# Linear attention and mixture of experts: one of four key-value products moved from GpSimd to VectorE, the second norm's statistics from VectorE to ScalarE

## The chip, the cores and the metric

The kernel runs on one core of a Trainium2 chip. The metric is the time of one execution on the device in microseconds (us), the median of several runs. The engines are TensorE (PE), VectorE (DVE), ScalarE (ACT), GpSimd (POOL) and SyncE (SP), which issues DMAs.

## The reference

The input x is 16 sequences of 512 tokens of width 128, in float32. Layer 0 is a state-space recurrence and a top-1 mixture of experts; layer 1 is linear attention and a top-2 mixture of experts. Both edits lie in layer 1's attention and in the norm behind it:

```python
h = _layernorm(x) * (1 + ca) + sa
q = softplus(h @ Wq.T + bq); k = softplus(h @ Wk.T + bk); v = h @ Wv.T + bv   # 16 heads of 8
kv  = cumsum(k[:, :, :, None] * v[:, :, None, :], axis=1)
k1  = cumsum(k, axis=1)
out = einsum('zsD,zsDe->zse', q, kv) / sum(q * k1)
x = x + ga * (out @ Wo.T + bo)
h = _layernorm(x) * (1 + cb) + sb          # the second norm
x = x + gb * moe(h)                        # top 2 of 8 experts
```

## The kernel before

The program has five phases, one behind the other: set-up and the first layer's norm and gate; the recurrence; layer 1's attention (about 345 to 705 us of the profiled execution), into which the first layer's results come; the expert phase (to about 925 us); and a last join, parts of which are laid into the expert phase. Everything below is about the attention phase.

A sequence `w` is cut into C = 4 chunks of 128 tokens. The phase is a software pipeline over sequences: each engine has a written-out loop over `n`, and each piece of work in it is a function of a sequence, such as `weighted(n - 1, 0)`. An engine executes strictly in that order; `need(engine, name, count)` is a wait on a semaphore. For each sequence:

- ScalarE normalises x (`norm0`), TensorE turns it (`turned`) and makes queries, keys and values; ScalarE and VectorE together make softplus out of absolute value, exponential, logarithm and two additions. VectorE's `softplus` (line 2007) is the last of these and sets the semaphore `qk`.
- For each chunk `c`, the outer products of keys and values, a tensor `kv` of 128 tokens x (8 x 128), are made by GpSimd in `products(w, c)` (line 1641). A ring of KB = 3 buffers (`kvb`) holds them. TensorE forms their running sums over tokens in `sums(w, c)` (line 2450, a product with a triangular matrix of ones), and VectorE multiplies these with q in `weighted(w, c)` (line 1983); TensorE's `reduced(w, c)` adds over heads.
- `states` (TensorE, line 2567) and `prefixes` (VectorE, line 2027) make the sums carried from chunk to chunk; `denominators` (VectorE, line 1989) the reciprocals; `divided` (line 1974) the attention output `g_t`.
- `projected` and `back` return it to token order, VectorE's `residual` (line 2032) adds it to x and sets `x3`.
- The second norm: VectorE's `moments` (lines 2038 and 2044) takes mean and variance with the batch-norm instructions, ScalarE's `variance_log` and `variance_root` make the reciprocal root (in `rv`), VectorE's `shifted` the product of minus the mean and it, ScalarE's `normed` (line 1821) applies both, VectorE's `modulated` (lines 2057, 2059) the modulation; `gated` and `added` (line 2070) put the norm's result into x.
- ScalarE's `squares` (line 1803), `payload` (lines 1715, 1717) and `turned_pay` (line 1834, output `p_t`) prepare the rows for the experts. TensorE's `logits_back` (line 2616), VectorE's `logits`, `largest` and `chosen` (lines 2076 to 2111) pick the two experts, and GpSimd's `send` (line 1650) writes rows to the experts' lists by indirect DMAs, eight for each sequence, laid between the products.

In VectorE's loop `chosen(n - 5)` stands right ahead of `corrected(n)` and `softplus(n)`, for which TensorE's `states(n - 1)` waits. TensorE lays idle products (line 70) into waits when the pipeline fills and drains. When the last sequences have drained, `front_counts` and `front_rows` on VectorE plan the first expert tiles, SyncE loads these rows, and TensorE goes on with the expert phase.

Of the kernel before, what the change touches and what calls it, by code (L numbers as in the profile page):

```python
# [16 lines left out]
P = 128  # L17
D = 128
C = 4
# [18 lines left out]
def build(nc, a, out):  # L38
# [9 lines left out]
    with ctx:  # L48
# [1232 lines left out]
        with ExitStack() as sc:  # L1281
# [17 lines left out]
            st = sb("st", [P, C, 6], scope=sc)  # L1299
            mv = [sb(f"mv{j}", [P, C, 2], scope=sc) for j in range(2)]  # L1300
# [46 lines left out]
                     "exp", "u1", "cor", "sub", "ln", "qk", "kv", "tri", "qc", "red", "k1", "qd", "st_ps", "ds", "skv", "den", "rden", "den_out", "spread0", "spread1",  # L1347
                     "att", "fold_ps", "fold", "folded", "wo", "wo_t", "wo_ps", "x3", "st", "mv", "lv", "rs", "sh", "me", "rm", "normed", "cb", "h4", "sq",
# [134 lines left out]
            with nc.Block() as block:  # L1483
# [142 lines left out]
                def _(pool):  # L1626
# [27 lines left out]
                    for n in range(B + 6):  # L1654
                        send(n - 6, 6)
                        products(n, 0)
                        send(n - 6, 7)
                        send(n - 5, 0)
                        products(n, 1)
                        send(n - 5, 1)  # L1660
                        send(n - 5, 2)
                        products(n, 2)
                        send(n - 5, 3)
                        products(n, 3)
                        send(n - 5, 4)
                        send(n - 5, 5)
# [14 lines left out]
                def _(act):  # L1681
# [3 lines left out]

                    def variance_log(w):
                        if exists(w):
                            need(act, "init", 3)
                            need(act, "mv", w + 1)
# [55 lines left out]
                    def relu_keys(w):  # L1745
                        if exists(w):
                            need(act, "k_ps", w + 1)
                            need(act, "kv", C * (w - 1))
# [4 lines left out]
                    def values(w):  # L1753
                        if exists(w):
                            need(act, "v_ps", w + 1)
                            need(act, "kv", C * (w - 1))
# [81 lines left out]
                    for n in range(4, B + 8):  # L1838
# [15 lines left out]
                        payload(n - 7)  # L1854
                        turned_pay(n - 7)
# [57 lines left out]
                def _(dve):  # L1913
# [70 lines left out]

                    def denominators(w):
# [48 lines left out]
                    def moments(w):  # L2034
                        if exists(w):
                            need(dve, "x3", w + 1)
                            for c in range(C):
                                last = nc.vector.bn_stats(st[:, c, :], tile(w, c))
                            last.then_inc(s["st"], 1)
                            need(dve, "st", w + 1)  # L2040
                            need(dve, "lv", w - 1)
                            need(dve, "sh", w - 1)
                            for c in range(C):
                                last = nc.vector.bn_aggr(mv[w % 2][:, c, :], st[:, c, :])
                            last.then_inc(s["mv"], 1)

                    def shifted(w):
                        if exists(w):
                            need(dve, "rs", w + 1)
                            need(dve, "normed", w - 1)  # L2050
                            nc.vector.scalar_tensor_tensor(sh[w % 2][:, :], mv[w % 2][:, :, 0], -1.0, rv[w % 2][:, :], ALU.mult, ALU.mult).then_inc(s["sh"], 1)
# [137 lines left out]
                    for n in range(B + 5):  # L2189
                        weighted(n - 1, 0)  # L2190
                        denominators(n - 1)
                        correction(n)
# [14 lines left out]
                        moments(n - 2)  # L2207
# [191 lines left out]
                def _(pe):  # L2399
# [386 lines left out]
```

## Time and profile before

| | |
|---|---|
| time, median of 3 runs | 938.53 us (938.17 to 942.1) |
| the profiled execution | 945.22 us, span 943.4 us |
| PE busy | 858.5 us, 91% |
| VectorE busy | 774.1 us, 82% |
| ScalarE busy | 618.2 us, 66% |
| GpSimd busy | 566.4 us, 60% |
| GpSimd's products, line 1641 | 64 of them, 127.3 us, mean 1995 ns |

The profile is one execution. A row of the timeline gives start and duration in us; the shares of busy time are averages over all five phases, and PE is nearly full in most of them. A wait is printed in square brackets at the end of the row that ended it, with the engine and line that released it.

### The profile page before, as it was taken

To read this page: it belongs to the slowest core of one execution; us is meant where nothing else is said; L and a number is where in the kernel's file an instruction comes from. 1 tells how busy PE (TensorE), PEld (TensorE's weight loads), DVE (VectorE), ACT (ScalarE), POOL (GpSimd) and SP (SyncE) were. 2 spreads that over 40 slices of the span, in tenths; PEclk is the share of its full clock that TensorE was granted. 3 is DMA by queue.
4 is the path that set the end of the run, shared out by engine and by line. 5 is a ranking of instruction groups with operands and counts; after the bars stand their busy time and mean duration, and the time that the engine had idled before them with its cause. 6 is when DMAs were issued, how large, how long until landed. Compare 5 with 4: busy or idle time off the path is not lost.

```text
span 943.4 us, 24125 instructions
## 1 busy us (share of the span) xinstructions
PE 858.5 (91%) x7676; PEld 674.7 (72%) x7692; DVE 774.1 (82%) x2369; ACT 618.2 (66%) x1603; POOL 566.4 (60%) x547
## 2 busy tenths in 40 slices
PE   6979898998999989999999999999879999999990
PEld 5945576645445458888778877787668888888890
DVE  3988787999999736988999999999886866666996
ACT  3557123487888446467677777666557888888880
POOL 1211004277776414443888888888777777777773
PEclk9989999899999999999999999999998999999996
DMA  5330262233223203001111112111227766756987
GB/s 155 95 95 1 67 204 59 104 110 141 102 101 130 99 3 96 15 17 35 43 52 49 49 54 64 53 50 49 66 68 219 219 183 183 228 181 196 338 263 248
DMA packets 93962, 105.82 MB, mean 112 GB/s; under 512 B 16095, under 2 KB 75802, under 8 KB 91661
## 3 DMA queue, kind: packets, MB, share of 16 engines
q1 hardware_dynamic: 81884, 84.59, 29.3%
q0 software_dynamic: 8640, 17.97, 5.3%
q10 hardware_dynamic: 3312, 1.70, 0.6%
q8 instruction: 64, 1.05, 0.5%
q14 instruction: 62, 0.50, 0.2%
HBM read 79.91 MB, written 24.32 MB: 110 GB/s over the span
## 4 chain that ended last, share of the span: by engine, by line
PE 48%; DVE 8%; issue 2%; ACT 2%; DMA 2%; POOL 1%; SPq 0%; ACTq 0%; DVEq 0%; POOLq 0%
PE ps L2694 12%; PE ps L2450 10%; PE ps L2717 6%; PE ps L2466 2%; PE ps L2513 2%; PE ps L2441 2%; PE ps L2416 2%; PE ps L2677 2%; PE ps L2567 2%; PE ps L2551 2%; PE ps L2429 1%; DVE qk L2001 1%; DVE qk L2007 1%; PE ps L2461 1%; DMA parts<-gx,dest 1%
## 5 line engine op out<-in xcount | busy, mean ns | idle before, releaser
L1641 POOL TENSOR_TENSOR kvb<-qk,v 128x1024 f32<-128x1024 f32 x64 | 127.3, 1995 | 68.8 <-DVE qk L2007 48.9
L1650 POOL DMA_INDIRECT rows_of<-payb,posu x128 | 144.3, 1128 | 40.1 <-issue 27.5
L2450 PE MATMUL ps<-con,kvb 128*128 128x128 f32 x1024 | 126.0, 276 | 0.0
L1161 PE MATMUL ps<-masked,ew 128*128 128x512 f32 x256 | 123.3, 610 | 1.9 <-DVE masked L1091 1.8
L2450 PEld LDWEIGHTS ps<-con,kvb 128*128 128x128 f32 x1024 | 119.4, 192 | 1.0 <-issue 1.0
L2378 DVE TENSOR_SCALAR qk<-ps,b 128x256 f32<-128x256 f32 x142 | 62.1, 478 | 49.7 <-PE ps L2694 44.6
L1674 POOL DMA_INDIRECT parts<-h,dest x72 | 80.6, 1119 | 23.3 <-issue 20.1
L1674 POOL DMA_INDIRECT parts<-gx,dest x70 | 78.7, 1125 | 21.3 <-issue 19.2
L1091 DVE TENSOR_TENSOR masked<-f_t,wide 128x512 f32<-128x512 f32 x128 | 85.9, 715 | 4.9 <-PE ps L1161 4.7
L1983 DVE TENSOR_TENSOR qc<-ps,qk 128x1024 f32<-128x1024 f32 x64 | 78.0, 1218 | 9.3 <-PE ps L2450 8.2
L1161 PEld LDWEIGHTS ps<-masked,ew 128*128 128x128 f32 x256 | 44.8, 192 | 44.9 <-issue 30.0
L2717 PE MATMUL ps<-w,f_t 128*128 x568 | 75.1, 275 | 0.0
L2717 PEld LDWEIGHTS ps<-w,f_t 128*128 128x128 f32 x568 | 69.0, 192 | 8.2
L1888 ACT ACTIVATE qk<-ps,b 128x256 f32<-128x256 f32 x142 | 59.6, 470 | 18.3 <-PE ps L2694 17.9
L2694 PE MATMUL ps<-qd,ex 128*128 128x256 f32 x288 | 69.8, 386 | 0.0
L2694 PE MATMUL ps<-qd,lg 128*128 128x256 f32 x280 | 66.2, 379 | 0.0
L70 PE MATMUL ps<-con 128*128 128x128 f32 x398 | 56.3, 293 | 5.5 <-PEq L75 3.9
L70 PEld LDWEIGHTS ps<-con 128*128 128x128 f32 x398 | 51.4, 204 | 9.6 <-issue 6.8
L2694 PEld LDWEIGHTS ps<-qd,ex 128*128 128x128 f32 x288 | 53.0, 194 | 6.0
L1893 ACT ACTIVATE nrm<-qk,limit 128x512 f32<-128x512 f32 x71 | 51.3, 722 | 6.8
L2267 DVE SCALAR_TENSOR_TENSOR f_t<-qk,nrm 128x512 f32<-128x512 f32 x71 | 49.2, 693 | 6.8 <-DVE qk L2378 0.5
L2694 PEld LDWEIGHTS ps<-qd,lg 128*128 128x128 f32 x280 | 50.5, 190 | 5.4
(370 smaller groups left out, 2107.0 us busy)
## 6 DMA issues: line engine op xcount, KB each, us to landing
wide<-hot_dram SPq DMA_DIRECT2D x16, 1024.0 KB, 4.6
kvb<-rows_of SPq DMA_DIRECT2D x71, 132.0 KB, 2.5
ex<-in_w_dram SPq DMA_DIRECT2D x36, 256.0 KB
lg<-in_w_dram SPq DMA_DIRECT2D x35, 256.0 KB
toep<-taps_dram SPq DMA_DIRECT2D x16, 512.0 KB, 4.5
xg<-parts SPq DMA_DIRECT2D x16, 512.0 KB, 5.2
x_tok<-in_x_dram SPq DMA_DIRECT2D x16, 256.0 KB, 2.9
rb<-den_dram SPq DMA_DIRECT2D x64, 64.0 KB
```

The costliest lines, as they stand in the source:

```text
L70: nc.tensor.matmul(ps[:, bank, 0:P], k("ident"), k("ident"), start=True, stop=True)
L1091: nc.vector.tensor_tensor(masked[e % 4][:, :], f_t[w % W][:, :], wide[w % W][:, e, :], ALU.mult).then_inc(s["masked"], 1)
L1161: nc.tensor.matmul(ps[:, w % 2, :], ew0[:, e, :], masked[e % 4][:, :], start=False, stop=(e == E - 1)).then_inc(s["product"], 1)
L1641: nc.gpsimd.tensor_tensor(kv[g % KB][:, :, :].rearrange("p e (h d) -> p e h d", h=H), k_in, v_in, ALU.mult).then_inc(s["kv"], 1)
L1650: nc.gpsimd.indirect_dma_start(rows_of, bass.IndirectOffsetOnAxis(ap=posu[w % PR][:, slot, t:t + 1], axis=0), pay[w % PB][:, t, :], None). ...
L1674: nc.gpsimd.indirect_dma_start(parts, bass.IndirectOffsetOnAxis(ap=dest[:, at, c:c + 1], axis=0), yw[u][:, c, :], None).then_inc(s_out[u], 16)
L1888: last = nc.scalar.activation(glu[v % 2][:, f, :], ps[:, bank, f * SP:(f + 1) * SP], ACT.Relu, bias=b1[:, bass.ds(e * NF + f, 1)], scale=-1.0)
L1983: nc.vector.tensor_tensor(qc[g % 2][:, :, :], cum(g), q_in, ALU.mult).then_inc(s["qc"], 1)
L2378: last = nc.vector.tensor_scalar(lin[v % 2][:, f, :], ps[:, bank + 1, f * SP:(f + 1) * SP], b1[:, bass.ds(e * NF + 2 + f, 1)], 8.0, ALU.ad ...
L2450: last = nc.tensor.matmul(cum(g)[:, e, :], kv[g % KB][:, e, :], k("upto"), start=True, stop=True)
L2694: last = nc.tensor.matmul(ps[:, bank + f // 2, (f % 2) * SP:(f % 2 + 1) * SP], w1c[v % WC][:, f * P:(f + 1) * P], x_t[v % 2][:, :], start= ...
L2717: last = nc.tensor.matmul(to, act_t[v % 2][:, j, c * P:(c + 1) * P], w2[:, bass.ds(e * (2 * D) + j * D, D)], start=False, stop=(c == S - 1 ...
```

## The change

GpSimd no longer makes the product of a sequence's fourth chunk. VectorE makes it in a new function `last_product(w)`, with a semaphore `kv_last` of its own, one round later in the loops' count, between `denominators` and `correction`. VectorE's `moments` is removed. In its place ScalarE gets three functions behind `payload` and ahead of `turned_pay`: `row_sums` (four copies that also give their sum), `negative_means` (one small scaling) and `centred_squares` (four squares of x minus mean that also give their sum, the bias being an operand by partition). `variance_log` and `shifted` read these results.

```diff
@@ GpSimd's loop
                         products(n, 2)
                         send(n - 5, 3)
-                        products(n, 3)
                         send(n - 5, 4)
...
@@ ScalarE
+                    def row_sums(w):
+                        if exists(w):
+                            need(act, "x3", w + 1)
+                            need(act, "nm", w)
+                            need(act, "vs", w)
+                            for c in range(C):
+                                last = nc.scalar.activation(unread[:, c, :], tile(w, c), ACT.Copy, accum_out=sx[:, c:c + 1])
+                            last.then_inc(s["sx"], 1)
+
+                    def negative_means(w):
+                        if exists(w):
+                            need(act, "sx", w + 1)
...
+                            nc.scalar.activation(nm[w % 2][:, :], sx[:, :], ACT.Copy, scale=-1.0 / D).then_inc(s["nm"], 1)
+
+                    def centred_squares(w):
+                        if exists(w):
+                            need(act, "nm", w + 1)
+                            need(act, "lv", w - 1)
+                            for c in range(C):
+                                last = nc.scalar.activation(unread[:, c, :], tile(w, c), ACT.Square, bias=nm[w % 2][:, c:c + 1], accum_out=vs[w % 2][:, c:c + 1])
+                            last.then_inc(s["vs"], 1)
...
-                            nc.scalar.activation(rv[w % 2][:, :], mv[w % 2][:, :, 1], ACT.Ln, bias=eps[:, :]).then_inc(s["lv"], 1)
+                            nc.scalar.activation(rv[w % 2][:, :], vs[w % 2][:, :], ACT.Ln, bias=eps[:, :], scale=1.0 / D).then_inc(s["lv"], 1)
...
                         payload(n - 7)
+                        row_sums(n - 5)
+                        negative_means(n - 5)
+                        centred_squares(n - 5)
                         turned_pay(n - 7)
                         norm0(n)
@@ VectorE
+                    def last_product(w):
+                        if exists(w):
+                            c = C - 1
+                            g = w * C + c
+                            need(dve, "qk", w + 1)
+                            need(dve, "v", w + 1)
+                            need(dve, "tri", g - KB + 1)
...
+                            nc.vector.tensor_tensor(kv[g % KB][:, :, :].rearrange("p e (h d) -> p e h d", h=H), k_in, v_in, ALU.mult).then_inc(s["kv_last"], 1)
...
                         weighted(n - 1, 0)
                         denominators(n - 1)
+                        last_product(n - 1)
                         correction(n)
                         weighted(n - 1, 1)
...
                         weighted(n - 1, 3)
-                        moments(n - 2)
                         first_cum(n)
@@ TensorE, in sums(w, c)
-                            need(pe, "kv", g + 1)
+                            if c == C - 1:
+                                need(pe, "kv_last", w + 1)
+                            else:
+                                need(pe, "kv", (C - 1) * w + c + 1)
```

The order of instructions on VectorE in one steady round, before, from the fourth product with q (`weighted(n - 1, 3)`) to the logits (`qd` is `first_cum`, `h` is `modulated`, `g_t` is `divided`, `rden` is `denominators`, `ex` is `correction`):

```order
L1983 TENSOR_TENSOR qc<-ps,qk 128x1024
L2038 BN_STATS st<-x_tok 128x6 x4
L2044 BN_AGGR mv<-st 128x2 x4
L2013 TENSOR_TENSOR qd<-ps,qk 128x512
L2070 TENSOR_TENSOR x_tok<-x_tok,gx 128x512
L2027 TENSOR_TENSOR skv<-skv 128x144 x2
L2057 TENSOR_TENSOR h<-h,rows 128x512
...
L1983 TENSOR_TENSOR qc<-ps,qk 128x1024
L1989 RECIPROCAL rden<-ps 96x128
L1994 SCALAR_TENSOR_TENSOR ex<-lg,ex 128x1024
L1983 TENSOR_TENSOR qc<-ps,qk 128x1024
```

And the same piece with the change, where line 2024 is the new product and the lines of the others have moved:

```order
L2013 TENSOR_TENSOR qc<-ps,qk 128x1024
L2054 TENSOR_TENSOR qd<-ps,qk 128x512
L2098 TENSOR_TENSOR x_tok<-x_tok,gx 128x512
L2068 TENSOR_TENSOR skv<-skv 128x144 x2
L2085 TENSOR_TENSOR h<-h,rows 128x512
...
L2013 TENSOR_TENSOR qc<-ps,qk 128x1024
L2030 RECIPROCAL rden<-ps 96x128
L2024 TENSOR_TENSOR kvb<-qk,v 128x1024
L2035 SCALAR_TENSOR_TENSOR ex<-lg,ex 128x1024
L2013 TENSOR_TENSOR qc<-ps,qk 128x1024
```

The eight small instructions of the moments are gone, and one large product stands between the reciprocal and the softplus correction. On ScalarE, the piece from the payload to `normed` (`h`), with the change:

```order
L1740 ACTIVATE payb<-h,rm 128x128 x4
L1742 ACTIVATE payb<-place 128x4
L1693 ACTIVATE unread,sx<-x_tok 128x128 x4
L1701 ACTIVATE nm<-sx 128x4
L1708 ACTIVATE unread,vs<-x_tok,nm 128x128 x4
L1861 ACTIVATE p_t<-ps 128x512
L1748 ACTIVATE nrm<-x_tok,shift,rs 128x128 x4
L1755 ACTIVATE ex<-ps,bq 128x512
L1848 ACTIVATE h<-x_tok,sh,rv 128x128 x4
```

Before, `p_t` followed directly on `payb<-place`; nine activations now stand between the two.

## Rows read from the trace of the kernel before

**Rows 1.** Chain of waits, 546 to 570 us: start, duration, what

```profile
550.55 0.97 PE ps L2567 x6
...
558.63 1.79 PE ps L2450 x16
...
565.49 0.12 PE ps L2616
...
569.51 1.24 DVE qk L2007
```

**Rows 2.** Timeline of VectorE, 546 to 570 us: start, duration, instruction

```profile
549.18 1.22 DVE L2007 TENSOR_TENSOR qk<-qk,lg 128x1024 f32<-128x1024 f32 x1
550.32 0.68 DVE L2032 TENSOR_TENSOR x_tok<-x_tok,ps 128x512 f32<-128x512 f32 x1
...
555.18 0.86 DVE L2038 BATCH_NORM_STATS2 st<-x_tok 128x6 f32<-128x128 f32 x4
...
556.37 0.66 DVE L2013 TENSOR_TENSOR qd<-ps,qk 128x512 f32<-128x512 f32 x1
556.95 0.93 DVE L2070 TENSOR_TENSOR x_tok<-x_tok,gx 128x512 f32<-128x512 f32 x1
...
558.36 0.68 DVE L2057 TENSOR_TENSOR h<-h,rows 128x512 f32<-128x512 f32 x1
...
560.46 1.23 DVE L1983 TENSOR_TENSOR qc<-ps,qk 128x1024 f32<-128x1024 f32 x1
...
562.46 1.16 DVE L1994 SCALAR_TENSOR_TENSOR ex<-lg,ex 128x1024 f32<-128x1024 f32 x1
564.12 1.22 DVE L1983 TENSOR_TENSOR qc<-ps,qk 128x1024 f32<-128x1024 f32 x1 [0.50 <-PE ps L2450]
565.64 0.19 DVE L2076 TENSOR_TENSOR logit<-ps,gb 128x32 f32<-128x32 f32 x1 [0.30 <-PE ps L2616]
...
566.27 0.25 DVE L2090 TENSOR_TENSOR wts<-top 128x4 f32<-128x4 f32 x1
```

**Rows 3.** Timeline of ScalarE, 546 to 570 us

```profile
549.74 0.19 ACT L1717 ACTIVATE payb<-place 128x4 f32<-128x4 f32 x1
553.91 0.60 ACT L1834 ACTIVATE p_t<-ps 128x512 f32<-128x512 f32 x1 [3.99 <-PE ps L2538]
...
556.52 1.64 ACT L1821 ACTIVATE h<-x_tok,sh,rv 128x128 f32<-128x128 f32 x4
...
564.68 0.30 ACT L1803 ACTIVATE junk<-h 128x128 f32<-128x128 f32 x1
...
564.97 0.30 ACT L1803 ACTIVATE junk<-h 128x128 f32<-128x128 f32 x1
```

**Rows 4.** Timeline of GpSimd, 546 to 570 us

```profile
555.33 1.99 POOL L1641 TENSOR_TENSOR kvb<-qk,v 128x1024 f32<-128x1024 f32 x1
...
560.05 1.98 POOL L1641 TENSOR_TENSOR kvb<-qk,v 128x1024 f32<-128x1024 f32 x1
562.20 2.28 POOL L1650 DMA_INDIRECT rows_of<-payb,posu  x1 [0.17 <-issue]
564.50 1.99 POOL L1641 TENSOR_TENSOR kvb<-qk,v 128x1024 f32<-128x1024 f32 x1
```

**Rows 5.** Timeline of VectorE and of TensorE, first sequence

```profile
373.37 1.23 DVE L2007 TENSOR_TENSOR qk<-qk,lg 128x1024 f32<-128x1024 f32 x1
...
374.74 0.97 PE L2567 MATMUL ps<-v,qk 128*128 128x144 f32 x6
```

**Rows 6.** Timeline of VectorE and ScalarE in the drain

```profile
681.27 0.68 DVE L2032 TENSOR_TENSOR x_tok<-x_tok,ps 128x512 f32<-128x512 f32 x1
...
683.29 1.64 ACT L1821 ACTIVATE h<-x_tok,sh,rv 128x128 f32<-128x128 f32 x4
...
685.12 0.68 DVE L2057 TENSOR_TENSOR h<-h,rows 128x512 f32<-128x512 f32 x1
```

**Rows 7.** Windows: busy us of PE, PEld, DVE, ACT, POOL; clock, DMA share, GB/s

```profile
705.00:710.00 5.00, 3.97 (x22) 3.34 (x21) 1.79 (x10) 0.99 (x2) 3.78 (x5) 0.68 0.79 227
```

More of the change, by code:

```diff
@@ L1298, in build @@
             rows = [sb(f"rows{u}", [P, 3, D], scope=sc) for u in range(W)]
-            st = sb("st", [P, C, 6], scope=sc)
-            mv = [sb(f"mv{j}", [P, C, 2], scope=sc) for j in range(2)]
+            sx = sb("sx", [P, C], scope=sc)
+            nm = [sb(f"nm{j}", [P, C], scope=sc) for j in range(2)]
+            vs = [sb(f"vs{j}", [P, C], scope=sc) for j in range(2)]
+            unread = sb("unread", [P, C, D], scope=sc)
             ms = [sb(f"ms{j}", [P, C], scope=sc) for j in range(2)]
@@ L1346, in build @@
             names = ("weights", "slots", "heads", "split", "init", "nrm0", "turned", "feat", "k_ps", "q_ps", "v_ps", "v", "abs_k", "abs_q", "relu_k", "relu_q",
-                     "exp", "u1", "cor", "sub", "ln", "qk", "kv", "tri", "qc", "red", "k1", "qd", "st_ps", "ds", "skv", "den", "rden", "den_out", "spread0", "spread1",
-                     "att", "fold_ps", "fold", "folded", "wo", "wo_t", "wo_ps", "x3", "st", "mv", "lv", "rs", "sh", "me", "rm", "normed", "cb", "h4", "sq",
+                     "exp", "u1", "cor", "sub", "ln", "qk", "kv", "kv_last", "tri", "qc", "red", "k1", "qd", "st_ps", "ds", "skv", "den", "rden", "den_out", "spread0", "spread1",
+                     "att", "fold_ps", "fold", "folded", "wo", "wo_t", "wo_ps", "x3", "sx", "nm", "vs", "lv", "rs", "sh", "me", "rm", "normed", "cb", "h4", "sq",
                      "pay", "pay_ps", "pay_t", "gx", "x4", "lg_ps", "lg_t", "lg_back", "lg", "max", "idx", "idf", "hot", "ed", "ee", "e1", "p1", "taken", "counted", "carried",
@@ L1747, in relu_keys @@
                             need(act, "k_ps", w + 1)
-                            need(act, "kv", C * (w - 1))
+                            need(act, "kv", (C - 1) * (w - 1))
+                            need(act, "kv_last", w - 1)
                             need(act, "st_ps", w - 1)
@@ L1755, in values @@
                             need(act, "v_ps", w + 1)
-                            need(act, "kv", C * (w - 1))
+                            need(act, "kv", (C - 1) * (w - 1))
+                            need(act, "kv_last", w - 1)
                             need(act, "st_ps", w - 1)
@@ L2032, in residual @@
                             nc.vector.tensor_tensor(seq(w), seq(w), ps[:, BACK, :].rearrange("p (c d) -> p c d", c=C), ALU.add).then_inc(s["x3"], 1)
[L2034 to L2045, printed above, removed]
                     def shifted(w):
@@ L2050, in shifted @@
                             need(dve, "normed", w - 1)
-                            nc.vector.scalar_tensor_tensor(sh[w % 2][:, :], mv[w % 2][:, :, 0], -1.0, rv[w % 2][:, :], ALU.mult, ALU.mult).then_inc(s["sh"], 1)
+                            nc.vector.tensor_tensor(sh[w % 2][:, :], nm[w % 2][:, :], rv[w % 2][:, :], ALU.mult).then_inc(s["sh"], 1)
                     def modulated(w):
```

6 lines of the change are left out of this document (5 added, 1 removed).

## The prediction

> **What bounds the kernel now.** The change touches only the attention phase, so I read the chain of waits there first, over one steady sequence [rows 1, 2]. It runs in a ring of two engines. VectorE finishes the softplus of a sequence (line 2007, at 549.18 and again at 569.51: a period of 20.33 us); TensorE, which has waited for it, starts at 550.55 and runs without a stop to its product of line 2616, which ends at 565.61 (15.06 us); VectorE takes the logits at 565.64 and needs 5.27 us until TensorE can start again. The sum is the period. TensorE and VectorE are thus both nearly full and neither is the bound alone: what counts is whether VectorE stands ready at 565.64.
>
> VectorE's own rows of that period [rows 2] show what room it has there. It takes the first product with q (line 1983) at 560.46, just behind the prefix sums that TensorE ended at 558.63 + 1.79 = 560.42, so that start is set by TensorE. It takes `ex` (line 1994) at 562.46 until 563.62, waits 0.50 us, takes the next line 1983 from 564.12 to 565.34, and waits 0.30 us for line 2616. Instructions that wait for nothing start 0.08 us before the end of the one before (line 2007 takes 1.22, and line 2032 starts 1.14 behind it), so each wait hides 0.08 more. The room is 0.50 + 0.30 + 2 x 0.08 = 0.96 us.
>
> **VectorE: the product it takes over.** `last_product` stands between the reciprocal and `ex`, inside that room. The trace has no such product on VectorE; the nearest row is line 2007, as many elements (128x1024 float32) with both inputs in SBUF: 1.22 us, 1.14 from start to start. Bounds: 1.07 (1.14 less the 0.07 by which such rows differ) and, if the inner broadcast cost as much as GpSimd's same product [rows 4], 1.98. I take 1.14, since line 1983 also reads a broadcast input at 1.23. The excess over the room is 1.14 - 0.96 = 0.18 us.
>
> **GpSimd: the product it loses.** It stood at 564.50 to 566.49 [rows 4]. VectorE's small subtraction of line 2090, two SBUF inputs, began at 566.27, took 0.25 and ended at 566.52, just behind it; where nothing of GpSimd's runs the same line takes 0.17. So the chain gets 0.08 us back. Nothing else waited for GpSimd there: TensorE uses this fourth product only in its next round. Steady cost: 0.18 - 0.08 = 0.10 us a period, over ten such periods 1.0 us. Bounds: with a product of 1.07 the cost is 0.03 us a period, 0.3 in all; with no cost at all the 0.08 would be a gain of 0.8; with 1.98 it is 1.98 - 0.96 - 0.08 = 0.94 a period, 9.4 us, which I leave out of the range, since line 1983's broadcast costs nothing to see.
>
> **VectorE: the moments it loses.** Start of line 2038 to start of line 2013 is 556.37 - 555.18 = 1.19 us [rows 2]. They would be a gain if VectorE set its own pace there, but behind them stands line 2070, two SBUF inputs. It already took 0.93 where a like op takes 0.68, ending at 557.88, 0.56 behind the end of GpSimd's second product at 555.33 + 1.99 = 557.32 [rows 4]. Without the moments it would stand ready at 555.76, wait for that same end and finish at the same 557.9. Line 2057 then starts at 558.36 as before, and the line 1983 at 560.46 waits for TensorE in any case. Worth: 0. I weighed a page here. The Trainium skill, page "SBUF — State Buffer", section "Who interferes with whom", says that a VectorE instruction with two SBUF inputs and a GpSimd instruction that reads SBUF hold one port in turn, one fully blocking the other. By it VectorE gains nothing from the moments' going; without it the 1.19 us would still be stopped by TensorE at 560.42. This trace agrees, in the 0.93 and the 0.25.
>
> **ScalarE: the statistics it takes over.** Its place is behind the payload copies, where it idles 3.99 us until 553.91 [rows 3]. The residual that it now needs ends at 550.32 + 0.68 = 551.00 [rows 2]. Four accumulating copies at the pace of line 1803 (564.68 to 564.97, 0.29 each) plus the last accumulator read: 1.26 us. One small scaling, as line 1717: 0.19, with 0.03 us of signal on either side. Four centred squares with a bias by partition: line 1821 has bias and scale by partition and goes at (1.64 - 0.10) / 4 = 0.385 each without an accumulator, line 1803 has neither and goes at 0.29 with one, of which the read is 0.09; half of 0.385 - 0.20 for the one operand gives 0.29 + 0.09 = 0.38 each, 1.52. Bounds for the four: 1.17 and 1.9. All together 3.04 us: 551.04 + 3.04 = 554.08, 0.17 behind the old 553.91. Line 1821 then ends at 558.16 + 0.17 = 558.33, and VectorE's line 2057 started at 558.36. Cost 0, cover 0.03 there and 0.10 more before 560.46; with 1.9 instead of 1.52 it would be about 0.25 us a period, 2.5 us. (The Trainium skill, page "ScalarE: Activation LUTs", section "What ACT_TABLE_LOAD costs", gives 93 ns for each operand by partition; by that the squares are 0.38 too.)
>
> **The first sequences** run at 18 us, TensorE being full. Only the first is tight: softplus ends at 374.60 and TensorE starts its next piece at 374.74 [rows 5]. VectorE waits 0.50 (+0.08) there, so 1.14 - 0.58 = 0.56 us is lost. In sequences two to five VectorE ends about 1 us early, but ScalarE's 3.04 us then stand in front of `norm0` and `normed`. I take 0.85 us for them together, by carrying 0.56 on; bounds 0 and 4 x 0.56. Sum 1.4 us.
>
> **The drain.** Behind the last sequence the pipeline empties in one chain, and ScalarE is on it. The last residual runs from 681.27 to 681.95; ScalarE's line 1821 for the sequence before starts at 683.29, and VectorE's line 2057, which waits for it, at 685.12 [rows 6]. Now the 3.04 us stand in between: 681.98 + 3.04 = 685.02, then p_t (0.5), line 1821 from 685.5 to 687.15, line 2057 at 687.2. That is 2.0 us later, and everything to the start of the expert phase hangs on it. The moments, 1.2 us of VectorE just ahead of 684.5, go, but ScalarE is the later of the two. One sequence earlier ScalarE idled and nothing is lost.
>
> **Sum.** 1.4 + 1.0 + 2.0 = 4.4 us. The profiled execution took 945.22 us with a span of 943.4; it becomes 949.6. It lies 6.7 us over the median of the three runs, 938.53; the shift goes over unchanged: **942.9 us**. A difference below 0.5% (4.7 us) can hardly be told from none, and this sum lies right under it.
>
> **Rivals.**
> 1. The clock falls in the drain. TensorE's granted clock was 0.68 in 705 to 710 [rows 7], shortly behind a wait of over 2 us. In the drain there is now a wait of 2.5 us, from about 683.2 to 685.7, where there was 0.33. If the clock goes to 1.2 GHz there, the 18 filler products (2.17 us, 0.97 us of idle behind them) take twice as long and push the chain by 1.2 us; a shifted fall at the start of the expert phase adds or takes up to 1.7. Against it: the clock was full all through 660 to 705 with gaps of 1 us. Time 944 to 946. Chance 0.17.
> 2. The steady period loses more than 0.1. Either the product on VectorE meets GpSimd's third product, which ends at 560.05 + 1.98 = 562.03, only 0.43 us ahead of its place at 562.46; or ScalarE is late by more than 0.30. Speaking for it: GpSimd's send at 562.20 took 2.28 us beside `ex`, against about 1 us, so such meetings occur. Each 0.3 us a period is 3 us: 946 to 950. Chance 0.16.
> 3. Other side: all is hidden. If VectorE's product costs 1.07 and TensorE's waits in the first sequences absorb the shift, only the drain is left, and there the moments' 1.2 us are partly gained: 938.5 to 940.5. Chance 0.15.
> 4. Faster: GpSimd sends without a pause behind 667. If its queue, 2 us shorter by a product, let the expert phase start its row writes earlier and these bounded the end, 936.5. Against it, TensorE runs that whole phase without a wait. Chance 0.04. That the change would leave the instructions as they were is excluded by their order.
>
> The sum's own case has 0.48, and 941.3 to 944.3 around it; about 0.17 of these 0.48 lies over 943.2 (938.5 + 4.7). So slower 0.17 + 0.16 + 0.17 = 0.50, faster 0.04 and within 0.46. The range takes the sum's case, the clock and half of rivals 2 and 3: 939.8 to 947.5.
>
> **What would show it.** The new trace should have VectorE's product at about 1.23 us; no wait ahead of the two q products behind it; steady softplus starts 20.43 us apart; `moments` gone and line 2070's successor waiting for GpSimd, some 1.5 us long; ScalarE's idle of 3.99 down to about 1.1 (up to the residual) and none at p_t; in the drain p_t near 2.2 us later against the residual than before. The prediction is wrong if the period falls below 20.3 or exceeds 20.7, or if the drain from the last softplus to the expert phase grows by less than 1 us or more than 4.

## The result, and the profile after

The changed kernel took 947.58 us, the median of 20 runs (941.21 to 955.18); the kernel before, run beside it, 941.31 us, also of 20 (938.17 to 949.8). The ratio is 1.0056 with a 95% interval of 1.0034 to 1.0077: 5.3 us slower, between 3.2 and 7.2. The two medians lie 6.3 us apart; all differences below are by the ratio, to which the interval belongs. The changed kernel's profiled execution took 943.13 us with a span of 941.3, less than the profiled one before. That is no gain of the change: attention began at 339.05 us in it against 345.05 before, so the phases ahead, which are the same code, ran 6.0 us shorter in that one execution. From there to the end it took 3.9 us longer. The kernel before was 938.53 us over the three runs that the prediction had, and 941.31 over twenty, so the forecast has to be read as a difference: 4.4 us over 938.53. The ratio on that base gives 943.8.

The shares of the page after (engine, busy us, instructions):

```profile
PE 853.6 (91%) x7676; PEld 672.9 (71%) x7692; DVE 787.3 (84%) x2257; ACT 665.6 (71%) x1875; POOL 556.0 (59%) x531
```

VectorE is 13 us busier although it lost the moments, ScalarE 47, and GpSimd only 10 less busy although 16 products of 2 us are gone. Windows tell more than the whole span. 460 to 560 us, kernel before, then after (busy us of PE, PEld, DVE, ACT, POOL; clock, DMA share, GB/s):

```profile
460.00:560.00 100.00, 94.55 (x1022) 79.71 (x1026) 93.81 (x260) 73.18 (x199) 85.51 (x60) 1.00 0.18 54
```

```profile
460.00:560.00 100.00, 93.92 (x1030) 79.48 (x1037) 98.03 (x220) 87.81 (x276) 85.27 (x55) 1.00 0.18 53
```

VectorE went from 93.8% to 98.0%. Its timeline of one period after, to be read against [rows 2] (start, duration, instruction):

```profile
551.70 2.10 DVE L2098 TENSOR_TENSOR x_tok<-x_tok,gx 128x512 f32<-128x512 f32 x1
...
554.38 0.69 DVE L2085 TENSOR_TENSOR h<-h,rows 128x512 f32<-128x512 f32 x1
...
556.38 1.23 DVE L2013 TENSOR_TENSOR qc<-ps,qk 128x1024 f32<-128x1024 f32 x1
557.52 0.94 DVE L2030 RECIPROCAL rden<-ps 96x128 f32<-96x128 f32 x1
558.38 1.16 DVE L2024 TENSOR_TENSOR kvb<-qk,v 128x1024 f32<-128x1024 f32 x1
559.46 1.21 DVE L2035 SCALAR_TENSOR_TENSOR ex<-lg,ex 128x1024 f32<-128x1024 f32 x1
560.59 1.21 DVE L2013 TENSOR_TENSOR qc<-ps,qk 128x1024 f32<-128x1024 f32 x1
561.73 0.18 DVE L2104 TENSOR_TENSOR logit<-ps,gb 128x32 f32<-128x32 f32 x1
...
562.35 0.17 DVE L2118 TENSOR_TENSOR wts<-top 128x4 f32<-128x4 f32 x1
```

No row has a bracket: the waits of 0.50 and 0.30 us are gone. The new product starts 1.08 us ahead of `ex`, and `ex`, which used to be followed by a wait, now takes 1.13 from start to start. The chain of waits says the same in its own way. Before it went to and fro between TensorE and VectorE [rows 1]; after, over the same stretch, it never leaves VectorE (start, length, what):

```profile
554.38 0.70 DVE h L2085
...
557.52 0.94 DVE rden L2030
558.46 1.08 DVE kvb L2024
559.54 1.13 DVE ex L2035
560.67 1.14 DVE qc L2013
...
565.55 0.42 DVE qk L2048
```

ScalarE's and TensorE's timelines after, against [rows 3] and the TensorE start in [rows 1]:

```profile
545.52 0.20 ACT L1742 ACTIVATE payb<-place 128x4 f32<-128x4 f32 x1
546.95 0.31 ACT L1693 ACTIVATE unread<-x_tok 128x128 f32<-128x128 f32 x1 [1.23 <-DVE x_tok L2073]
...
548.26 0.20 ACT L1701 ACTIVATE nm<-sx 128x4 f32<-128x4 f32 x1
548.50 0.40 ACT L1708 ACTIVATE unread<-x_tok,nm 128x128 f32<-128x128 f32 x1
...
550.05 0.58 ACT L1861 ACTIVATE p_t<-ps 128x512 f32<-128x512 f32 x1
```

```profile
546.47 0.97 PE L2598 MATMUL ps<-v,qk 128*128 128x144 f32 x6 [1.02 <-DVE qk L2048]
```

The statistics take 546.95 to 550.05, 3.10 us. Counted from TensorE's start, `p_t` came at 553.91 - 550.55 = 3.36 before and comes at 550.05 - 546.47 = 3.58 now: 0.22 late, and without a wait.

GpSimd after, against [rows 4]:

```profile
551.26 1.98 POOL L1643 TENSOR_TENSOR kvb<-qk,v 128x1024 f32<-128x1024 f32 x1
...
558.12 3.41 POOL L1652 DMA_INDIRECT rows_of<-payb,posu  x1 [0.17 <-issue]
...
564.39 1.95 POOL L1652 DMA_INDIRECT rows_of<-payb,posu  x1 [0.30 <-issue]
```

The drain after, against [rows 6], ScalarE, VectorE and TensorE; then the windows' row of 683 to 686:

```profile
682.34 0.57 ACT L1861 ACTIVATE p_t<-ps 128x512 f32<-128x512 f32 x1
682.82 1.63 ACT L1848 ACTIVATE h<-x_tok,sh,rv 128x128 f32<-128x128 f32 x4
684.55 0.69 DVE L2085 TENSOR_TENSOR h<-h,rows 128x512 f32<-128x512 f32 x1 [3.26 <-ACT h L1848]
683.06 0.66 PE L2635 MATMUL ps<-p_t,gw 128*32 128x128 f32 x8 [2.59 <-ACT p_t L1861]
```

```profile
683.00:686.00 3.00, 2.94 (x19) 2.59 (x20) 1.41 (x3) 2.01 (x7) 2.39 (x3) 0.50 0.17 51
```

The last residual starts at 678.53, so line 2085 follows it by 6.02 us, against 685.12 - 681.27 = 3.85 before.

### The profile page after: what moved, and what is told of

It is laid out like the page before. It is cut to its first block, busy times and chain, and to the rows that moved or that the text cites. A ratio compares the mean times of both kernels' runs of the same rounds, so it can differ in the third digit from the quotient of the medians.

```text
span 941.3 us, 24269 instructions
## 1 busy us (share of the span) xinstructions
PE 853.6 (91%) x7676; PEld 672.9 (71%) x7692; DVE 787.3 (84%) x2257; ACT 665.6 (71%) x1875; POOL 556.0 (59%) x531
## 4 chain that ended last, share of the span: by engine, by line
PE 31%; DVE 22%; issue 4%; ACT 3%; DMA 2%; SPq 0%; POOL 0%; DVEq 0%; ACTq 0%; POOLq 0%
PE ps L2725 13%; PE ps L2748 6%; DVE qc L2013 4%; PE ps L2481 3%; DVE x_tok L2098 2%; DVE qk L2042 2%; PE ps L2708 2%; DVE ex L2035 2%; DVE kvb L2024 1%; DVE rden L2030 1%; DVE qk L2048 1%; PE ps L2497 1%; DVE h L2085 1%; DVE idx L2120 1%; DMA parts<-gx,dest 1%
## 5 line engine op out<-in xcount | busy, mean ns | idle before, releaser
L1652 POOL DMA_INDIRECT rows_of<-payb,posu x128 | 165.9, 1296 | 42.6 <-issue 29.6
L1643 POOL TENSOR_TENSOR kvb<-qk,v 128x1024 f32<-128x1024 f32 x48 | 95.0, 1988 | 80.4 <-DVE qk L2048 79.8
L1918 ACT ACTIVATE qk<-ps,b 128x256 f32<-128x256 f32 x142 | 59.7, 471 | 16.5 <-PE ps L2725 15.9
```

The lines of the kernel that those rows point to most:

```text
L1643: nc.gpsimd.tensor_tensor(kv[g % KB][:, :, :].rearrange("p e (h d) -> p e h d", h=H), k_in, v_in, ALU.mult).then_inc(s["kv"], 1)
L1652: nc.gpsimd.indirect_dma_start(rows_of, bass.IndirectOffsetOnAxis(ap=posu[w % PR][:, slot, t:t + 1], axis=0), pay[w % PB][:, t, :], None). ...
L1918: last = nc.scalar.activation(glu[v % 2][:, f, :], ps[:, bank, f * SP:(f + 1) * SP], ACT.Relu, bias=b1[:, bass.ds(e * NF + f, 1)], scale=-1.0)
```

## The experiments

To compare executions whose clock fell at different moments I cut each trace at the same instructions of the attention phase. The table is worked out from the timelines; each kernel has 4 to 12 runs behind its ratio (the changed one 20), beside 11 to 28 of the kernel before. **Five** is from the first softplus to the sixth. **Period** is a tenth of the time from the sixth to the sixteenth. **Drain** is from the last residual's start to the start of the `modulated` line behind it. For the whole periods between 450 and 680 us, per period: **waits** of VectorE and of TensorE on another engine, and **held**, which adds up, over VectorE's instructions, what each took beyond the shortest duration that the same one has in any of these traces, where that is over 0.1 us.

| kernel | five | period | drain | V waits | V held | T waits | median us | ratio (95%) |
|---|---|---|---|---|---|---|---|---|
| before | 88.45 | 20.35 | 3.85 | 0.80 | 0.39 | 0.92 | | |
| after | 89.74 | 20.47 | 6.02 | 0.00 | 1.56 | 1.04 | 947.58 | 1.0056 (1.0034 to 1.0077) |
| e1 | 90.04 | 20.47 | 6.03 | 0.00 | 1.56 | 1.04 | 945.05 | 1.0043 (1.0019 to 1.0068) |
| e2 | 89.78 | 20.47 | 3.86 | 0.00 | 0.42 | 1.06 | 943.81 | 1.0022 (0.9990 to 1.0054) |
| e3 | 89.13 | 20.35 | 6.03 | 0.80 | 1.56 | 0.92 | 944.82 | 1.0056 (1.0026 to 1.0087) |
| e4 | 90.07 | 20.47 | 3.83 | 0.00 | 1.56 | 1.04 | 947.85 | 1.0082 (1.0053 to 1.0112) |
| e5 | 88.46 | 20.25 | 6.03 | 0.80 | 1.57 | 0.82 | 942.14 | 1.0003 (0.9972 to 1.0034) |
| e6 | 96.54 | 24.63 | 6.03 | 2.24 | 2.11 | 3.32 | 993.47 | 1.0517 (1.0457 to 1.0577) |
| e7 | 86.04 | 29.97 | 5.32 | 6.73 | 4.38 | 8.44 | 1047.35 | 1.1145 (1.1096 to 1.1193) |
| e8 | 87.93 | 28.56 | 6.04 | 5.46 | 4.52 | 7.45 | 1029.61 | 1.0945 (1.0901 to 1.0988) |
| e9 | 85.98 | 22.59 | 3.86 | 0.42 | 3.34 | 2.18 | 967.21 | 1.0271 (1.0228 to 1.0313) |
| e10 | 88.74 | 22.93 | 6.03 | 0.21 | 3.84 | 2.27 | 971.63 | 1.0310 (1.0269 to 1.0351) |
| e11 | 86.72 | 22.47 | 6.04 | 0.65 | 3.84 | 2.04 | 965.32 | 1.0247 (1.0208 to 1.0286) |
| e12 | 90.06 | 23.08 | 6.03 | 0.45 | 4.13 | 2.65 | 972.59 | 1.0316 (1.0272 to 1.0360) |

For the kernels in the old order a second table cuts the same traces at two more places. **Last** is from the sixteenth softplus to the last residual, **packed** from that `modulated` line to the packed places (`packs`, VectorE's last step in planning the first expert tiles), **all** from the first softplus to the packed places.

| kernel | last | packed | all | against before |
|---|---|---|---|---|
| before | 30.41 | 16.95 | 343.16 | |
| after | 31.15 | 16.88 | 348.52 | +5.36 |
| e1 | 29.72 | 17.10 | 347.59 | +4.43 |
| e2 | 29.99 | 16.87 | 345.18 | +2.02 |
| e3 | 30.34 | 16.85 | 345.80 | +2.64 |
| e4 | 29.67 | 20.00 | 348.25 | +5.09 |
| e5 | 29.58 | 16.88 | 343.44 | +0.28 |

### e1_both, e2_product_only, e3_stats_only: the two parts apart

e1 is the changed kernel again. e2 keeps VectorE's product and gives VectorE its moments back; e3 keeps ScalarE's statistics and gives GpSimd its fourth product back.

```diff
  e2, ScalarE and VectorE          e3, GpSimd and VectorE
-     row_sums(n - 5)            +     products(n, 3)
-     negative_means(n - 5)      -     last_product(n - 1)
-     centred_squares(n - 5)
+     moments(n - 2)
```

> The changed kernel once more, beside the runs below. Theory: the attention phase alone grows, by parts that are the same in every execution: first sequences +0.5 to 1, ten steady periods of 20.45 us against 20.33 (+1.2), the drain +2.1; what lies over that is the granted clock, which falls at other places in each execution. So the softplus starts stand 20.45 apart again, and the time from the last residual to VectorE's modulation in the drain is 6.0 us against 3.85. Rival: the 6.0 us of the last drain were the fall of the clock seen there, and come out near 4 where the clock stays full.

> Only the product moves from GpSimd to VectorE; the moments stay on VectorE. Theory (a port wait takes the place of the moments, and TensorE sets the start of the first product with q anyway): the same period of 20.45, the first sequence +0.55, the drain as before (3.85 us from the last residual to the modulation); in all +1.5 to 2.5 us. Rival (the moments' 1.19 us are a real gain on VectorE that pays for the product): a period near 21.4 and over +10 us.

> Only the statistics move from VectorE to ScalarE; the product stays on GpSimd. Theory: period 20.33 unchanged although VectorE has 1.2 us less to do, first sequences +0.3 to 0.8 by norm0 and normed behind the statistics, drain +2.1; in all +2.5 to 3. Rival (VectorE's load sets the period): below 20.0 us a period, over 3 us faster in all.

The traces separate the parts more sharply than the times do. The product alone makes the whole 0.12 us of the period and 1.3 us of the first five sequences, and leaves the drain as it was. The statistics alone leave the period exactly as it was, cost 0.7 us in the first five and 2.2 us in the drain. Together the three stretches come to 1.3 to 1.6, 1.2 and 2.2, about 4.8 us. The last sequences give some back: "last" is 0.7 us shorter than before in e1. It is shorter wherever GpSimd makes no fourth product and the clock stays full (29.58 to 29.99 in e1, e2, e4 and e5, but 30.34 in e3). In all e1's trace is 4.43 us longer, and the parts alone 2.02 + 2.64 = 4.66. Beside them stand the measured 5.3 (3.2 to 7.2) and, for e1, 4.0 (1.8 to 6.4). The parts don't add up stretch by stretch: in the first five sequences e2 loses 1.33 us and e3 0.68, and both together 1.29 and 1.59. So e1 lost more there than the 0.5 to 1 that I expected, and e2 more than 0.55.

The trace after shows a price that e1's does not. TensorE waits 1.45 us for the last softplus in it and 1.46 in e1. Windows' rows just behind that wait, after and then e1:

```profile
649.00:651.00 2.00, 2.00 (x11) 1.91 (x11) 1.87 (x4) 1.70 (x10) 1.84 (x2) 0.50 0.00 0
```

```profile
651.00:653.00 2.00, 2.00 (x21) 2.00 (x20) 1.97 (x10) 1.94 (x12) 1.84 (x2) 1.00 0.00 0
```

The granted clock fell to 0.50 in one and stayed full in the other, with the same kernel, and "last" is 31.15 us against 29.72. So 1.4 of the 5.36 us of the trace after go with a fall of the clock that came in one execution and not in the other.

The statistics also settle what became of the moments. VectorE's second norm sum, in the groups by line of 460 to 620 us, e2 (moments there) and e3 (moments gone), each: count | busy, mean ns of one | idle before:

```profile
L2082 DVE TENSOR_TENSOR x_tok<-x_tok,gx 128x512 f32<-128x512 f32 x7 | 6.5, 935 | 0.0
```

```profile
L2097 DVE TENSOR_TENSOR x_tok<-x_tok,gx 128x512 f32<-128x512 f32 x8 | 16.8, 2104 | 0.0
```

It grew by 1.17 us when 1.19 us ahead of it went. In the trace after it stands over GpSimd's product of 551.26 to 553.24 and ends at 553.80, 0.56 us behind that product's end, as before. This is the rule that the prediction weighed (the Trainium skill, "SBUF — State Buffer", section "Who interferes with whom"), and e3 bears out the hold. Whether TensorE's prefix sums would have stopped the gain without it, as the prediction also says, no run separates.

### e4_drain_fixed: the statistics elsewhere in the drain

```diff
-                        row_sums(n - 5)
-                        negative_means(n - 5)
-                        centred_squares(n - 5)
+                        if n < B + 3:
+                            statistics(n - 5)
                         turned_pay(n - 7)
...
                         normed(n - 6)
+                        if n >= B + 3:
+                            statistics(n - 5)
```

> The changed kernel, but for the last two sequences ScalarE makes the statistics behind normed instead of ahead of p_t. Theory: the drain goes back to 3.9 to 4.2 us from the last residual to the modulation, everything behind it about 2 us earlier; the steady period stays 20.45; in all +2 to 3.5 us against before. Rival (the drain's length is the clock's or TensorE's): no change against the changed kernel.

`modulated` came back to 3.83 us behind the residual, but the stretch from there to the packed places was 20.00 us against 16.88 after: the same 3 us of ScalarE now stand ahead of its logit transpose. Nothing was won: the whole is +5.09 us against e1's +4.43, not 2 us less as expected, and the measured 7.7 us (5.0 to 10.5) says no better. In both places that I tried in the drain, ScalarE's queue is the path.

### e5_no_fourth, e6_two_products: no product, and two

```diff
  e5                                    e6, in last_product
-     last_product(n - 1)             +     nc.vector.tensor_tensor(again[w % 2] ..., k_in, v_in, ALU.mult)
                                            nc.vector.tensor_tensor(kv[g % KB] ..., k_in, v_in, ALU.mult)
```

> This kernel is the changed one with the fourth product made by no engine. TensorE's cumulative sums of every sequence's last chunk read what the buffer held before, so the output leaves out that chunk's own key-value products; every other instruction stands. Theory (the product on VectorE costs its own 1.08 us at a point of the ring, where all but some 0.96 us of it is hidden): softplus starts come 20.25 to 20.35 us apart (changed kernel 20.47, kernel before 20.35), so 0.12 to 0.22 less per period, and the first sequences win back the 0.5 to 1.3 us that the product alone took. In all 2 to 4 us less than the changed kernel, about 941 to 943 us. Rival (what costs is not the product but GpSimd's changed order of sends and products, or ScalarE's statistics): the periods stay 20.45 to 20.5.

> The changed kernel with VectorE's product made twice, the second time into a buffer that nothing reads. Theory (the room behind the product is used up by the first one, so that VectorE's further work lengthens the ring one for one): the period grows by the product's own 1.08 to 1.13 us, to 21.55 to 21.6 from 20.47, and the kernel is 16 to 19 us slower than the changed one, about 962 us. Rival (room left, the 0.12 us of the changed kernel come from meetings with GpSimd's work): the period grows by 0.1 to 0.5 us only, 2 to 8 us in all.

e5 came out as expected: 20.25. Without any fourth product VectorE's waits are back (0.80 a period), and the period is 0.10 below that of the kernel before, which is the small subtraction that GpSimd's fourth product used to hold up. So the two steady terms stand apart: e3 to e5 is GpSimd's product going, -0.10; e5 to e1 is VectorE's product coming, +0.22. In its first five sequences e5, with the statistics, loses nothing (88.46); the 0.68 us of e3 come only with GpSimd's fourth product beside them.

e6 missed by far. I expected 1.1 us a period and got 4.16. The second product took its 1.1, and everything behind it moved against GpSimd and ScalarE. Timeline of VectorE, then of TensorE, in e6, and its windows' row of 463 to 682:

```profile
587.10 2.95 DVE L2087 TENSOR_TENSOR h<-h,rows 128x512 f32<-128x512 f32 x1 [1.19 <-ACT h L1849]
```

```profile
577.81 1.78 PE L2600 MATMUL ps<-v,qk 128*128 128x144 f32 x6 [3.24 <-DVE qk L2050]
```

```profile
463.00:682.00 219.00, 187.94 (x1841) 159.21 (x1838) 194.04 (x413) 159.51 (x502) 162.48 (x99) 0.91 0.15 44
```

The sum of `modulated` now waits for ScalarE and is then held for 2.3 us by GpSimd's product; held time grew by 0.55 us a period against the changed kernel. TensorE waited 3.24 us in one piece, and the mean clock was 0.91 where it was 1.00 before. The line behind that wait took 1.78 us instead of 0.97. Of the 4.16 us, 1.1 are the product, 0.55 is held time, and the other 2.5 go with new waits and the lower clock, which I did not take apart. VectorE, "full" at 98%, did not simply get longer by what was added.

### e7_ring_before, e8_ring_after: a new order

```diff
@@ VectorE, from the logits on
+ corrected(n)  softplus(n)  residual(n - 2)  weighted(n - 1, 2)  states(n)  shifted(n - 3)  weighted(n - 1, 3)
  largest(n - 5)  chosen(n - 5)  gated(n - 4)  ...  modulated(n - 3)
+ ranked(n - 5)  placed(n - 5)
@@ TensorE
- states(n - 1)  ranks(n - 6)  sums(n - 2, 3)
+ states(n - 1)  sums(n - 2, 3)  ...  reduced(n - 2, 3)  ranks(n - 6)  keys(n)
```

> The kernel before with its loop's steps in another order: VectorE does the corrections, softplus, residual, weighting and shifts ahead of the choice of experts, ScalarE's weighing stands behind the queries' relu, TensorE's rank product behind the third reduction, GpSimd's sends one place later. What is computed is the same. Theory (the period is a ring of 15.06 us of TensorE and 5.27 us of VectorE, and part of VectorE's share is work that nobody in the ring waits for): the period falls to what TensorE's own work makes it, 19.3 to 19.8 us, and the kernel is 7 to 16 us faster, 925 to 934 us. Rival (VectorE's and GpSimd's load, or the sends' new places, hold the period): it stays 20.2 to 20.5 and the time within 3 us of the kernel before, or grows, if a new wait ends up in the ring.

> The same new order with both parts of the change in it. Theory (the change costs because its product lies in the ring): with the ring shorter than VectorE's and TensorE's own work, the product costs nothing or gains a little, 0 to 0.1 us a period against the same order without the change, and what is left is ScalarE's statistics in the drain, about 2 us: 0 to 3 us slower than that kernel. Rival (VectorE is the next to set the period, busy near 17 us of 20): the change costs 0.5 us or more per period there too, 5 us or more in all beside the drain's 2 us.

Neither theory: 30 us a period. In e7's trace TensorE waits twice:

```profile
569.54 0.18 PE L2586 MATMUL ps<-taken,earlier 128*128 128x32 bf16 x1 [3.58 <-DVE upto_now L2107]
574.61 0.61 PE L2414 MATMUL ps<-bk,one 128*128 128x512 bf16 x1 [4.87 <-DVE rank L2120]
```

I had moved the choice of experts behind work that nobody waited for, but TensorE's rank product stood ahead of its keys, and the keys need the bank that VectorE's `rank` empties. The ring became nearly all of both engines in turn. e8 is still of use: in that order the change gains 1.4 us a period (29.97 to 28.56), because VectorE's moments stood in the ring there and the product in VectorE's waiting time. That account is read from the order and the waits (VectorE's went from 6.73 to 5.46 us a period); no run took the two parts of the change apart in this order.

### e9_swap_before, e10_swap_after, e11_swap_stats: a smaller exchange

```diff
@@ VectorE                         @@ TensorE               @@ GpSimd: sends one product later
- largest(n - 5)  chosen(n - 5)    - ranks(n - 6)           - send(n - 6, 6) ahead of products(n, 0)
  corrected(n)  softplus(n)          sums(n - 2, 3)         + send(n - 6, 6), send(n - 6, 7) behind it
+ largest(n - 5)  chosen(n - 5)    + ranks(n - 6)           + send(n - 5, 0) behind products(n, 1) ...
```

> The kernel before with three places exchanged, the computation the same: VectorE makes the corrections and softplus ahead of the largest logits and the choice of experts, TensorE's rank product stands behind the fourth cumulative sums instead of ahead of them, and GpSimd's sends stand one product later. Unlike the first new order, the choice stays ahead of everything that TensorE waits for next. Theory (a ring of 15.06 us of TensorE and 5.27 us of VectorE, of which about 2.4 us are the choice, which the ring needs not): TensorE's 0.9 us wait ahead of the states goes, and the period falls from 20.35 to what either engine has of its own work, 20.33 - 0.89 = 19.4 of TensorE and 20.33 - 0.80 = 19.5 of VectorE: 19.5 to 19.8 us, the kernel 8 to 14 us faster than the one before. Rival (the exchange puts a wait in another place, as the first new order did): 20.3 us or more, no faster.

> The changed kernel with the same three places exchanged. Theory one (the product costs by its place in the ring): once the ring is loosened, it costs next to nothing, the period is 19.5 to 19.9 and the kernel 8 to 14 us faster than the changed one. Theory two (VectorE is full: in the changed kernel it is 98% busy from 460 to 560 us and waits for nobody, so that its own 20.4 us set the period, not the ring): the exchange takes nothing off, the period stays 20.2 to 20.5, and the kernel is 10 us or more slower than the one before with the exchange.

> The kernel before with the statistics by ScalarE alone, the fourth product on GpSimd, and the same three places exchanged. Theory (VectorE's floor is 19.5 us less the 1.24 us of the moments, so TensorE's 19.4 us are next): a period of 19.4 to 19.6, up to 0.2 us below that of the kernel before with the exchange, 0 to 3 us less in all, of which the 2.2 us that the statistics cost in the last sequences go off again. Rival (what the moments leave on VectorE is lost to the lock with GpSimd's product, as at the second norm's sum in the kernel before's order): the same period as the kernel before with the exchange, and 2 us slower in all.

TensorE's wait for softplus did go, and the first five sequences became 2.5 us shorter (88.45 to 85.98). But the period rose to 22.6. Groups by line in e9, 460 to 620 us, VectorE and TensorE:

```profile
L2070 DVE TENSOR_TENSOR x_tok<-x_tok,gx 128x512 f32<-128x512 f32 x7 | 15.2, 2178 | 0.0
L2090 DVE TENSOR_TENSOR wts<-top 128x4 f32<-128x4 f32 x7 | 12.3, 1755 | 0.2
```

```profile
L2538 PE MATMUL ps<-con,payb 128*128 128x128 f32 x32 | 5.6, 301 | 17.0 <-DVE rank L2120 17.0
```

The subtraction of line 2090, four elements a partition, now meets GpSimd's first product and takes 1.76 us instead of 0.17; the norm's sum 2.18. VectorE is held 3.3 us a period, its `rank` comes late, and TensorE waits for it 17.0 us in eight periods. With the change, or its statistics alone, in that order (e10, e11) the periods are 22.93 and 22.47, outside every range that I had given, and the times within 5 us of e9's. The hold only moved: in e11 the norm's sum takes 0.68 us, and the prefix additions behind it, which also read SBUF twice, are held instead:

```profile
L2067 DVE TENSOR_TENSOR skv<-skv 128x144 f32<-128x144 f32 x14 | 18.3, 1304 | 0.2
```

A pair of them takes 2.64 us where it is 0.64 elsewhere. Taking the moments away gained 0.12 us a period (22.59 to 22.47), and VectorE is held 3.84 us in e10 and e11 against 3.34 in e9.

### e12_second_early: GpSimd's second product one send earlier

```diff
                         send(n - 6, 7)
-                        send(n - 5, 0)
                         products(n, 1)
+                        send(n - 5, 0)
```

> The changed kernel with GpSimd's second product one send earlier, ahead of the send that waits for the places; nothing else is touched. In the changed kernel this product lies over VectorE's sum behind the second norm (x_tok with gx, both in SBUF), which takes 2.10 us there instead of about 0.68. Theory (VectorE is full and its own work, this hold of 1.4 us in it, sets the period of 20.47): the product ends before the sum starts, the sum takes 0.7 to 1.0 us, VectorE's waits come back (0.5 to 1.4 us a period), and the period is the ring's again, 20.25 to 20.35: 1.2 to 2.2 us less in ten periods and 2 to 4 us less in all. Rival (the product on VectorE adds to the ring by its place, whatever else VectorE does): the sum shortens but the period stays at 20.45 to 20.5.

The sum behind the second norm fell to what was expected, and the period rose all the same. VectorE in e12, 460 to 620 us:

```profile
L2098 DVE TENSOR_TENSOR x_tok<-x_tok,gx 128x512 f32<-128x512 f32 x7 | 4.7, 675 | 0.0
...
L2163 DVE SCALAR_TENSOR_TENSOR payb<-wts,payb 128x4 f32<-128x4 f32 x7 | 17.3, 2475 | 0.0
...
L2085 DVE TENSOR_TENSOR h<-h,rows 128x512 f32<-128x512 f32 x7 | 13.3, 1901 | 2.3 <-ACT h L1848 2.3
```

The product no longer holds the sum (0.68 us); in its new place it holds a four-element instruction that writes the payload (2.48 us), and `modulated` (1.90). 4.13 us a period are held where it was 1.56, and TensorE's waits rose from 1.04 to 2.65. Neither the expected 20.25 to 20.35 nor the rival's 20.45 to 20.5 came out. Whether a full VectorE or the product's place made the 0.12 us can't be read from this run, since the hold was only moved and grew.

## Why the prediction was right

**The ring and its room** (15.06 + 5.27, with 0.96 us of room) were read rightly. e5, which has neither fourth product, waits 0.80 us again and runs at 20.25; e2 and e1 wait nowhere.

**VectorE's product**, 1.14 us predicted, measured 1.08 from start to start (near the lower bound of 1.07); but `ex` behind it went from 1.08 to 1.13, and a copy (line 2124) from 0.17 to 0.23. The excess over the room, 0.18 predicted, was 0.22 by e5 against e1. **GpSimd's relief**, 0.08, was 0.10 by e3 against e5, and line 2118 takes 0.17 where line 2090 took 0.25. Net 0.12 a period for 0.10, 1.2 us for 1.0.

**The moments were worth nothing**: the period of e3 is that of before, to 0.01 us. It is the point at which counting busy time would have gone wrong, since VectorE's list was shortened by 1.19 us and its day was not. What I had expected from [rows 2], an instruction of 1.5 us, was one of 2.10: the moments' whole time came back in it. The prediction's own working, ready at 555.76 and finished at 557.9, already made it 2.1; its 1.5 does not follow from it.

**ScalarE's statistics**: 3.10 us for 3.04, `p_t` 0.22 late for 0.17, squares 0.385 from start to start for 0.38, cost in the steady period 0, as said. The four squares go at the sum of this trace's own terms, and the 93 ns of the Trainium skill's "ScalarE: Activation LUTs", section "What ACT_TABLE_LOAD costs", agrees with 0.385 - 0.29.

**The first sequences**: 1.4 predicted, 1.3 and 1.6 in the two traces. TensorE's new wait in the first is the 0.56 us predicted:

```profile
368.95 0.97 PE L2598 MATMUL ps<-v,qk 128*128 128x144 f32 x6 [0.55 <-DVE qk L2048]
```

The rest was not where I put it, and the nearness of the sum is luck. The product alone (e2) makes 1.33 us: the interval from the second softplus to the third, in which I had given VectorE about 1 us of room, went from 17.16 to 18.30 in e2 and in the trace after, the product's whole length. The statistics alone (e3) leave that interval as it was and make 0.68.

**The drain**: 2.0 predicted, 2.17 measured, by ScalarE alone (e3 has it, e2 has not), on the way that was described. From the last softplus to the packed places the whole is 51.21 us before, 54.05 after and 52.85 in e1: longer by 2.84 and 1.64, inside the 1 to 4 that the prediction set. The sum had no term for the stretch ahead of the last residual, which is 0.7 us shorter in e1, and 1.4 longer again in the trace after, with the clock.

**The rivals.** The clock of the first did fall in the drain, to 0.50 in the row of 683 to 686, behind TensorE's wait of 2.59 us. There it cost nothing: from `modulated` to the packed places it is 16.88 us, as in e2 (16.87). In e1, where the rows of 683 to 690 have 0.77 and 0.75, it is 17.10. What the rival has right is that the clock can lengthen the end: the fall behind the last softplus took 1.4 us in the trace after, and none in e1, though it is not the place that I named. The other half of that rival, a shifted fall at the start of the expert phase, belongs to the execution: from the packed places to TensorE's first bias product of the experts' second layer (line 2712, 2743 after) it was 15.5 us before and 13.4 after, and between 13.4 and 15.9 in e1 to e5. So a single execution can hide a good part of 4 or 5 us. The second rival happened only in kernels that I made (e6, e9, e12). The third, that only the drain would be left and partly paid back, is excluded by the period and the first sequences, and the fourth by the ratio.

The sum of 4.4 us stands beside 4.43 in e1's trace and 5.3 (3.2 to 7.2) in the runs. The mechanism was right in the steady periods and the drain; that the whole agrees so closely is partly luck, since the first sequences lost their time elsewhere and the last ones gave back 0.7 us that I had not counted. The margin was weak too. "No difference" had a chance of 0.46 and "slower" 0.50, because the sum lay just under the 4.7 us bound, and the two measurements lie on either side of it (5.3 and 4.0). As an absolute time 942.9 was less good: the median of twenty is 947.58, just over the range's 947.5, because the three runs that it was counted from lay 2.8 us under the twenty.

What stays open: e3's time (5.3 us slower, 2.4 to 8.2) is more than the 2.64 us that its trace shows; the interval reaches down to that. And whether another order would let the change pay: none that I tried beats the kernel before.

## What to carry to other kernels

When an engine is nearly full in a tuned ring, take away work only after looking at what stands behind it: if the next instruction has two SBUF inputs and lies over a GpSimd product, it waits for the same end, and the gain is nothing. Cost an added instruction by the waits that it fills, from start to start, and look at a moved one again in the emptying pipeline at the end, where 2.17 us of ScalarE's 3.10 were on the path that cost nothing in a steady period. And distrust any new order: here each of three (e7, e9, e12) lengthened the period by over 2 us, and in each an instruction of four or eight elements had come over a GpSimd product of 2 us.

## What the hardware showed that I had not expected

- GpSimd's product holds an instruction of four elements a partition as long as a large one: 0.15 to 0.17 us became 1.76 (e9) and 2.48 (e12). Two details: in e12 and e7 such an instruction starts 0.5 us ahead of the product's own row, so it can be held longer than the 1.98 us of the product; and one that is held for 2.22 us in e7, the cast of the expert numbers (line 2096), has a single input.
- The hold goes the other way too. A send of GpSimd's, 0.96 to 1.0 us alone, took 2.28 beside `ex` [rows 4], 3.41 beside product and `ex`, and 1.95 beside one softplus line. The first two are as if it had waited for those instructions (0.98 + 1.16 = 2.14, and 0.98 + 1.16 + 1.21 = 3.35); that was not tried by itself. So the 2 us that GpSimd was spared came back in its sends: per period, products went from 7.91 to 5.93 us and sends from 9.52 to 11.51. In e5, where VectorE makes no product either, the sends take 9.39, so the 2 us come with VectorE's product. This is why its busy share stood still at 85%.
- Two engines at 94 and 98% are not "full plus a bit": 1.1 us more on VectorE cost 4.16 us in e6, and the granted clock went from 1.00 to 0.91 with TensorE's waits of over 3 us.
